# Layer 1's gate operations over four steps, gathers that wait for one another, and experts' sums added in two places

## What is computed

```
# layer 0, ffn: eight experts; each takes the 512 tokens of 4096 with the highest scores for it
top_scores, sel = top_k(softmax(xt @ wg).T, 512)
routed = xt[sel] * top_scores                     # gather
out = zeros.at[sel].add(silu(routed @ w1[e]) * (routed @ w3[e]) @ w2[e])   # scatter-add

# layer 1, attention: 16 heads of 64, causal with a window and 64 global tokens
# layer 1, ffn: eight experts, each token takes the two best by gate
scores = sigmoid(xf @ gate_w.T);  sel = top_k(scores + expert_bias, 2)
out = sum_e  w_e * square(relu(xf*w_e @ wu[e].T)) @ wd[e].T     # w_e = score of e if e is in sel, else 0
```

## Time and profile before

| | |
|---|---|
| median of 3 runs (lowest, highest) | 2264.98 us (2264.29, 2267.79) |
| profiled execution | 2265.04 us, its span 2263.2 us |
| PE, PEld | 2043.8 us busy (90%), 1546.9 (68%) |
| DVE | 1461.5 us (65%) |
| ACT | 1159.4 us (51%) |
| POOL | 895.9 us (40%) |
| layer 0 to about 439 us, layer 1 to 1270 us | |

### The profile page before, as it was taken

The page is one execution under the profiler, slowest core; times in us unless marked ns, Lnnn a source line. Parts: engine busy times, 40 slices in busy tenths (PEclk is TensorE's granted clock), DMA queues, the critical chain, the costliest instruction groups (busy, mean ns, idle before and its releaser), DMA issues.

```text
span 2263.2 us, 47747 instructions
## 1 busy us (share of the span) xinstructions
PE 2043.8 (90%) x15692; PEld 1546.9 (68%) x15692; DVE 1461.5 (65%) x5301; ACT 1159.4 (51%) x3600; POOL 895.9 (40%) x1416
## 2 busy tenths in 40 slices
PE   5887977399999999999999899999997999999998
PEld 2555644277777777777777566666665777777776
DVE  6999843366666666666666655555556777777776
ACT  3443342155455555555554455555545666666665
POOL 3113255345455444444444411111114545454554
PEclk9887779689999999999999899999998999999999
DMA  6000016600000000000000000000000000000001
GB/s 190 8 1 1 8 34 159 173 2 1 2 2 1 1 2 1 2 2 1 2 2 1 1 0 0 0 0 0 0 0 1 2 2 2 2 2 1 2 1 39
DMA packets 37479, 36.86 MB, mean 16 GB/s; under 512 B 5648, under 2 KB 34448, under 8 KB 36368
## 3 DMA queue, kind: packets, MB, share of 16 engines
q1 hardware_dynamic: 31632, 29.82, 4.2%
q0 software_dynamic: 5632, 4.33, 1.4%
HBM read 23.53 MB, written 10.62 MB: 15 GB/s over the span
## 4 chain that ended last, share of the span: by engine, by line
PE 67%; issue 11%; DVE 8%; ACT 8%; POOL 4%; DMA 1%; DVEq 0%; SPq 0%; another core or an unknown queue 0%; POOLq 0%; ACTq 0%
PE bank L1313 7%; PE bank L1302 6%; PE bank L1241 5%; PE bank L1288 4%; PE bank L1285 4%; PE bank L1335 4%; PE bank L1226 2%; PE bank L1228 2%; PE bank L1227 2%; ACT work L1373 2%; PE bank L1700 2%; PE bank L1722 2%; PE bank L1305 2%; PE bank L1234 2%; PE bank L1724 2%
## 5 line engine op out<-in xcount | busy, mean ns | idle before, releaser
L1596 POOL TENSOR_TENSOR work<-work 128x128 f32<-128x128 f32 (+1 forms) x1048 | 503.6, 512 | 698.5 <-DVE work L1496 698.5
L1373 ACT ACTIVATE work<-work 128x128 f32<-128x128 f32 x524 | 206.7, 395 | 546.0 <-DVE work L1484 546.0
L1491 DVE COPY work<-bank 128x384 f32<-128x384 f32 x520 | 283.6, 550 | 26.5 <-PE bank L1313 11.1
L1374 ACT ACTIVATE work<-work 128x256 f32<-128x256 f32 x524 | 258.6, 493 | 0.0
L1313 PE MATMUL bank<-w_const,work 128*128 128x128 f32 x1560 | 228.9, 283 | 1.0 <-POOL work L1596 1.0
L1484 DVE CUSTOM_DVE_ANT_0 work<-bank,mask 128x256 f32<-128x256 f32 x524 | 220.0, 420 | 0.0
L1313 PEld LDWEIGHTS bank<-w_const,work 128*128 128x128 f32 x1560 | 166.9, 141 | 47.5 <-issue 43.1
L1517 DVE COPY work<-bank 128x512 f32<-128x512 f32 x136 | 93.5, 687 | 158.7 <-PE bank L1236 152.1
L1483 DVE CUSTOM_DVE_ANT_0 work<-bank,mask 128x128 f32<-128x128 f32 x524 | 151.0, 288 | 53.6 <-PE bank L1288 49.1
L1302 PE MATMUL bank<-work 128*64 128x256 f32 x1032 | 171.7, 410 | 4.4 <-DVE work L1517 4.0
L1226 PE MATMUL bank<-l_xn_hi,l_qk_hi 128*128 128x256 f32 x532 | 163.6, 308 | 2.9 <-DVE l_xn_lo L1437 2.8
(11 more groups left out here) (338 smaller groups left out, 4934.2 us busy)
## 6 DMA issues: line engine op xcount, KB each, us to landing
w_l<-in_l SPq DMA_DIRECT2D x1, 3210.5 KB, 10.4
w_l<-in_l SPq DMA_DIRECT2D x2, 1540.0 KB
w_f<-in_f SPq DMA_DIRECT2D x1, 3072.0 KB, 13.9
x_sb<-in_x SPq DMA_DIRECT2D x4, 512.0 KB, 6.0
normed_rows<-work SPq DMA_DIRECT2D x1, 2048.0 KB, 9.3
even_experts<-x_sb SPq DMA_DIRECT2D x8, 256.0 KB, 3.6
residual<-x_sb SPq DMA_DIRECT2D x1, 2048.0 KB, 9.7
qk<-in_qk SPq DMA_DIRECT2D x2, 1024.0 KB
```

The source lines that it names most:

```text
L1373: act.activation(pr[g % 4][:, Q0], pr[g % 4][:, Q0], ACT.Exp, scale=-1.0, bias=nmx[:, g % 4, 0:1], accum_out=sm[:, g % 4, 0:1])
L1374: act.activation(pr[g % 4][:, Q1], pr[g % 4][:, Q1], ACT.Exp, scale=-1.0, bias=nmx[:, g % 4, 1:2], accum_out=sm[:, g % 4, 1:2]).then_inc(s ...
L1491: dve.tensor_copy(pt[g % 4], PS[2 + g % 2][:, 0:384]).then_inc(s_te.s, 1)
L1596: ins = pool.tensor_tensor(w, w, spread(rc[:, g % 4, q:q + 1], w.shape[1]), ALU.mult)
```

## The change

**Gates.** The ten gate operations, all in step 8 (and 16) before, become a function `gates(i, n, part)` with four parts, called in steps 8, 9, 10 and 11 (and 16 to 19). Part 0: L1522 to L1524. Part 1: L1527, L1528. Part 2: L1529, L1530. Part 3: L1531 to L1534. The operations and the waits between them are the same.

**Gathers.** `gathered(e)` waits for group e - 1 to land, for all e from 1 on.

**Experts' sums.** `acc_back` is now three pieces, of 9, 9 and 14 tiles, at other places in `work`; `acc_d` and `res_d` are each loaded in three DMAs of these sizes. SyncE waits for `b_y` = 8 as well before it loads `acc_d`. VectorE adds piece 0 in layer 0's phase, and pieces 1 and 2 in layer 1's preparatory part, behind `rest(0)` and before the preparatory steps.

```diff
             def gathered(e):
-                if e >= 3:
-                    pool.wait_ge(b_got[e % 3], 16 * CT * (e // 3))
+                if e >= 1:
+                    pool.wait_ge(b_got[(e - 1) % 3], 16 * CT * ((e + 2) // 3))
...
-        acc_back = xg_cols[:, 0:TILES * D]
+        ACC_TILES = ((0, 9), (9, 18), (18, TILES))
+        acc_back = [work[:, at:at + (b - a) * D].rearrange("p (t d) -> p t d", d=D) for at, (a, b) in zip((6144, 1812, 4096), ACC_TILES)]
...
-            dve.wait_ge(acc_in, 16)
-            for c in range(4):
-                dve.wait_ge(x_back[c], 16)
-                dve.tensor_tensor(x_sb[:, 8 * c:8 * c + 8, :], x_sb[:, 8 * c:8 * c + 8, :],
-                                  acc_back[:, 1024 * c:1024 * c + 1024].rearrange("p (t d) -> p t d", d=D), ALU.add).then_inc(x_sum, 1)
-            dve.wait_ge(x_sum, 4)
+            experts_added(dve, 0)
+            dve.wait_ge(x_sum, 1)
+
+        def experts_added(dve, c):
+            a, b = ACC_TILES[c]
+            dve.wait_ge(acc_in, 16 * len(ACC_TILES))
+            dve.wait_ge(x_back[c], 16)
+            dve.tensor_tensor(x_sb[:, a:b, :], x_sb[:, a:b, :], acc_back[c], ALU.add).then_inc(x_sum, 1)
...
             sp.wait_ge(b_xs, E0)
+            sp.wait_ge(b_y, E0)
             sp.wait_ge(b_added[0], 16 * CT * E0 // 2)
-            sp.dma_start(acc_back.rearrange("p (t d) -> p t d", d=D), acc_v).then_inc(acc_in, 16)
+            for c, (a, b) in enumerate(ACC_TILES):
+                sp.dma_start(acc_back[c], acc_v[:, a:b, :]).then_inc(acc_in, 16)
             sp.wait_ge(b_added[1], 16 * CT * E0 // 2)
             sp.wait_ge(b_acc, 16)
-            for c in range(4):
-                sp.dma_start(x_sb[:, 8 * c:8 * c + 8, :], res_v[:, 8 * c:8 * c + 8, :]).then_inc(x_back[c], 16)
+            for c, (a, b) in enumerate(ACC_TILES):
+                sp.dma_start(x_sb[:, a:b, :], res_v[:, a:b, :]).then_inc(x_back[c], 16)
...
                 rest(0)
+                if moe:
+                    for c in range(1, len(ACC_TILES)):
+                        experts_added(dve, c)
+                    dve.wait_ge(x_sum, len(ACC_TILES))
...
+                def gates(i, n, part):
+                    w = wt2[n % 2]
+                    other, own = spread(bi.unsqueeze(2), 2, E1, E1), spread(bi.unsqueeze(3), 2, E1, E1)
+                    sq = lambda v: v.rearrange("p t (e j) -> p t e j", j=E1)
+                    if part == 0:
+                        dve.wait_ge(*read(i, "g", n))
+                        mark(dve.tensor_scalar(sg, ex, 1.0, None, ALU.add)); settle(i)
+                        mark(dve.reciprocal(sg, sg)); settle(i)
+                        mark(dve.tensor_tensor(bi, sg, spread(L["eb"].unsqueeze(1), 2, E1), ALU.add)); settle(i)
+                    if part == 1:
+                        mark(dve.tensor_tensor(sq(cgt), other, own, ALU.is_gt))
+                        mark(dve.tensor_tensor(sq(ceq), other, own, ALU.is_equal)); settle(i)
+                    if part == 2:
+                        mark(dve.tensor_tensor(ceq, ceq, spread(C["tri8"].unsqueeze(1), 2, E1 * E1), ALU.mult)); settle(i)
+                        mark(dve.tensor_tensor(cgt, cgt, ceq, ALU.add)); settle(i)
+                    if part == 3:
+                        mark(dve.tensor_reduce(rk, sq(cgt), AX, ALU.add)); settle(i)
+                        dve.wait_ge(f_x.s, f_x.at(i, E1 * (n - 1) - 1))
+                        mark(dve.scalar_tensor_tensor(w, rk, 1.5, sg, ALU.is_lt, ALU.mult)); settle(i)
+                        dve.tensor_tensor(w, w, w, ALU.mult).then_inc(g_w.s, 1)
...
                     for at, kind, n in MISC:
...
-                        if at != s or kind not in "vg":
-                            continue
-                        if kind == "v":
+                        if kind == "g" and at <= s < at + 4:
+                            gates(i, n, s - at)
+                        if at == s and kind == "v":
...
-                        if kind == "g":
```

More of the change, by code:

```diff
@@ L900, in program @@
         hh = [in_xnT(2, 512) for _ in range(2)]
-        acc_back = xg_cols[:, 0:TILES * D]
+        ACC_TILES = ((0, 9), (9, 18), (18, TILES))
+        acc_back = [work[:, at:at + (b - a) * D].rearrange("p (t d) -> p t d", d=D) for at, (a, b) in zip((6144, 1812, 4096), ACC_TILES)]
         b_acc, acc_in, x_sum = sem("b_acc"), sem("even_experts_in"), sem("x_sum")
-        x_back = [sem(f"x_back{c}") for c in range(4)]
+        x_back = [sem(f"x_back{c}") for c in range(len(ACC_TILES))]
         l1_half = sem("in_l1_half")
@@ L1517, in step @@
                             dve.tensor_copy(v_sb[p][:, t, half_ * 512:(half_ + 1) * 512], PS[BANK["v"]][:, :]).then_inc(empty_(kind), 1)
-                        if kind == "g":
-                            w = wt2[n % 2]
-                            dve.wait_ge(*read(i, kind, n))
-                            mark(dve.tensor_scalar(sg, ex, 1.0, None, ALU.add)); settle(i)
-                            mark(dve.reciprocal(sg, sg)); settle(i)
-                            mark(dve.tensor_tensor(bi, sg, spread(L["eb"].unsqueeze(1), 2, E1), ALU.add)); settle(i)
-                            other, own = spread(bi.unsqueeze(2), 2, E1, E1), spread(bi.unsqueeze(3), 2, E1, E1)
-                            sq = lambda v: v.rearrange("p t (e j) -> p t e j", j=E1)
-                            mark(dve.tensor_tensor(sq(cgt), other, own, ALU.is_gt))
-                            mark(dve.tensor_tensor(sq(ceq), other, own, ALU.is_equal)); settle(i)
-                            mark(dve.tensor_tensor(ceq, ceq, spread(C["tri8"].unsqueeze(1), 2, E1 * E1), ALU.mult)); settle(i)
-                            mark(dve.tensor_tensor(cgt, cgt, ceq, ALU.add)); settle(i)
-                            mark(dve.tensor_reduce(rk, sq(cgt), AX, ALU.add)); settle(i)
-                            dve.wait_ge(f_x.s, f_x.at(i, E1 * (n - 1) - 1))
-                            mark(dve.scalar_tensor_tensor(w, rk, 1.5, sg, ALU.is_lt, ALU.mult)); settle(i)
-                            dve.tensor_tensor(w, w, w, ALU.mult).then_inc(g_w.s, 1)
                     u = s - 5
```

## The result

| | before | after |
|---|---|---|
| median (lowest to highest) | 2265.57 us (2264.29 to 2267.79), 4 runs | 2209.15 us (2205.53 to 2211.15), 4 runs |
| ratio, 95% interval | | 0.9749 (0.9737 to 0.976) |
| profiled execution | 2265.04, span 2263.2 | 2205.53, span 2203.7 |
| PE busy | 2043.8 us | 2009.0 us |
| mean granted clock | 0.942 | 0.961 |

The account below looks back on a forecast made before the run. TensorE, busy 90% of the span, was taken as the bound, so edits pay only where it waits. 2265.0 - 29.1 (gates) - 7.2 (clock) - 4.8 (experts' sums) = 2224 us, gathers at zero; range 2217 to 2236 us.

Parts of the forecast that it names:

- Gates over four steps: Layer 1's loop: three of four gate parts hide in VectorE's idle time, saving 1.82 us in 16 half passes, 29.1 us.
- The leak: Layer 1's steps 9 to 11: gates slowed beside GpSimd; priced zero, up to 0.7 us per half pass (2235 us, chance 0.12).
- GpSimd shuts the gates out: Rival, layer 1's loop: gate operations start only once GpSimd has no more work, delaying copies; 2271 us, chance 0.04.
- The clock: Layer 1's steps behind gate steps: shorter TensorE stops no longer lower the clock, gaining 7.2 us (ends 0 and 7.2).
- Experts' sums: Hand-over from layer 0 to layer 1: adding nine tiles first, the other two adds hidden, starts layer 1 4.8 us earlier.
- Gathers: Layer 0: GpSimd's new waits before gather groups delay no key block; price zero, upper end 4 us of cost.

Follow-up runs that it names:

- third job: The changed kernel measured once more on a third chip, where the kernel before took 2240.79 us: 2202.29 us, ratio 0.9832.
- plain loads: Kernel before with GpSimd's gathers replaced by SyncE's eight plain transfers of the same bytes, routing left out: 2243.07 us, ratio 0.9923, on a chip with stops.

## Why the prediction was wrong, and where it was right

**Gates over four steps: right.** 8.46 - 6.65 = 1.81 us, where 1.82 was forecast. That the parts are free because they stand ahead of the copy, in VectorE's idle time, was an argument from the earlier trace rows; with the parts behind the copy 1.03 of the 1.18 us of parts 1 and 2 come back in steps 9 and 10. That part 3 needs the place ahead of the copy no run shows. What stays in the loop is part 0, and moving it one step on took 0.64 us out of step 8.

**The leak: right in kind.** Beside GpSimd's work the gate operations take longer: L1533 before, which is L1499 after (ns, shortest, median, longest):

```profile
L1533 DVE SCALAR_TENSOR_TENSOR work<-work x17: 174/175/176, 451.3 to 1243.3; 128x16 f32<-128x16 f32 x17
```
```profile
L1499 DVE SCALAR_TENSOR_TENSOR work<-work x17: 174/470/473, 442.1 to 1203.7; 128x16 f32<-128x16 f32 x17
```

By their means L1491, L1492, L1495 and L1499 take 0.11, 0.19, 0.08 and 0.28 us more, 0.66 in a half pass; 1.4 had been allowed. The idle time takes it in: steps 9 and 10 are 0.05 and 0.07 us longer than forecast, 1.9 us in all. The rival in which GpSimd shuts the gates out did not happen: no copy of steps 9 to 11 waited for a gate operation. Its chance of 0.04 rested in part on a misreading, though. The prediction says that the trace of before shows no price as large as a GpSimd operation, and it does (VectorE's and GpSimd's timeline; L484 takes 0.26 us elsewhere):

```profile
272.61 1.29 POOL L323 TENSOR_TENSOR w_l<-work,w_const 76x512 f32<-76x512 f32 x1
272.70 1.25 DVE L484 TENSOR_SCALAR w_l<-w_const,w_l 128x76 f32<-128x76 f32 x1
```

L484 ends at 273.95, when GpSimd's operation does (273.90). In the loop the same seems to go on with shorter operations: L1499, at 916.25 in after, ends at 916.72, and GpSimd's L1609 beside it at 916.69. The rival failed because GpSimd's operations there end soon enough, not because VectorE never waits for them.

**The clock: right.** No step of the loop has a clock below 1.00 in after or with the gates alone. Stops of 0.56 and 0.77 us in a row don't lower it here. By the steps behind a gate step it gives back 110.68 - 16 x 6.52 = 6.4 us of the 7.2.

**Experts' sums: right**, 5.0 us by the trace (4.8 forecast), 3.4 (1 to 5) by the runs of that part alone. The last scatter's landing kept its time: from the end of the last issue to SyncE's release 411.61 - 406.61 = 5.0 us, 5.07 before. Three DMAs for one changed nothing there.

**Gathers: the step that failed.** The prediction said "Price zero", with ends 0 and 4 us, all on the costly side; the edit measured 15.5 us less alone and some 19 less within the change. As a cost the price was right: GpSimd's waits are 12.0 us in all, and on a chip without stops the edit measures 1.0005. What it did not ask is what the *rows of issues* cost the other engines in the kernel before. It looked at GpSimd's own rows and at what is queued behind the wait, and no further; the "remote" waits of ScalarE, PE's "issue" of 4.75 us and the clock of 0.81 stood in the same stretch of the trace. Those rows don't say what makes the stops, but they give the size of what such an edit might take away: 9.6 us of ScalarE's stops and 2.9 of VectorE's, plus what the low clock behind them costs. That the result fell below the range is this step alone: with the old gathers' wait the change measures 2227.59. It also hung on the chip: by the ratio of the third job, 0.9832, a kernel of 2265 us comes to 2227, within the range. Its opening sentence, that an edit elsewhere pays only where PE waits, was applied to layer 1's loop alone.

**The mechanism, as far as it is shown.** Shown: PE's signals are counted late beside gathers that GpSimd issues; cutting the rows at all seven places takes away ScalarE's "remote" stops and 15 to 19 us, and plain loads in their place take away every late signal and 17.4 us. This happens in the jobs where the kernel before takes 2260 to 2266 us and not in those where it takes 2241 to 2242, and there the edit is worth nothing. Not shown: why the signals come late, whether it is the chip that decides it, and why an edit at one or two places moves a stop instead of ending it.

The remaining 3.1 us (phase borders, later layers) were not forecast and not tested.

## What to carry to other kernels

Price an added wait on both sides: besides who waits for the waiting engine, look at what all engines did while that engine ran without pause, and above all at waits which the profile can put down to nothing ("remote", a long "issue") and at the clock behind them. When a wait has cured something, hold it against a kernel that has none of the trouble at all; here the plain loads showed how much the wait had left. To hide work on an engine that waits inside a loop, put it ahead of the instruction that waits; the same work behind that instruction is paid nearly in full where the loop closes through it (1.03 of 1.18 us here). A gain that rests on such stops can be there on one chip and absent on the next, so compare on more than one.

## What the hardware showed that was not expected

- Beside rows of indirect DMA issues on GpSimd, signals of PE can come late: its product ended at 316.18 us and was counted at 320.69. The kernel before differs by 18 to 25 us between the two kinds of job, with the program unchanged.
- An operation of 16 columns with two SBUF operands went from 0.175 to 0.47 us beside GpSimd (L1499 above), and one of a single column from 0.16 to 2.62 us. VectorE's and GpSimd's timeline in after:

```profile
285.44 2.62 DVE L483 TENSOR_TENSOR w_l<-w_l 128x1 f32<-128x1 f32 x1
285.69 0.70 POOL L317 TENSOR_TENSOR w_l<-qk,w_const 128x304 f32<-128x304 f32 x1
286.34 1.09 POOL L323 TENSOR_TENSOR w_l<-qk,w_const 76x512 f32<-76x512 f32 x1
287.39 0.63 POOL L341 TENSOR_TENSOR x_sb<-x_sb,work 128x256 f32<-128x256 f32 x1
288.09 0.26 DVE L484 TENSOR_SCALAR w_l<-w_const,w_l 128x76 f32<-128x76 f32 x1
```

It ends at 288.06, when GpSimd's third operation does (288.02), though its own record starts ahead of the first, while a gather was being issued. That VectorE and GpSimd share a port pair as an exclusive lock, so that the one that comes later is fully blocked, is what the Trainium skill states ("SBUF — State Buffer", section "SBUF: two separate sides"). The trace agrees that VectorE waits to the end of GpSimd's work, here and for L484 in the trace of before; here the wait lasted through three operations in a row. In the loop of layer 1 the price stayed at 0.08 to 0.28 us for an operation.
